# Last edge stage of a four-layer graph network: 144 of its columns built on TensorE instead of 112

## The reference

```
W = jnp.einsum('rb,bio->rio', comp, basis)
msg = node_feats[src] * norm
seg = etype.astype(jnp.int32) * N + dst
s = jax.ops.segment_sum(msg, seg, num_segments=R * N)
h = jnp.einsum('rni,rio->no', s.reshape(R, N, -1), W) + bias
```

## Time and profile before

| | us |
|---|---|
| median of 3 runs (lowest, highest) | 4992.75 (4991.7, 4993.47) |
| profiled execution, its own time | 4994.97 |
| its span, first to last instruction | 4992.8 |
| PE busy | 3904.1 (78%) |
| DVE busy | 4035.4 (81%) |
| ACT busy | 2091.6 (42%) |
| POOL busy | 3669.7 (73%) |
| POOL gathers from `rel_tab`, 672 | 643.1 busy, 205.0 idle in front of them |

### The profile page before, as it was taken

How to read it: one execution, slowest core, us unless ns; L and a number is a source line. 1 busy time by engine, 2 the same in 40 slices (tenths; PEclk the granted TensorE clock), 3 DMA queues, 4 the chain that set the end, 5 groups by cost and what they waited for, 6 DMA issues and landing times. The chain is left out here.

```text
span 4992.8 us, 56860 instructions
## 1 busy us (share of the span) xinstructions
PE 3904.1 (78%) x17000; PEld 2737.1 (55%) x17049; DVE 4035.4 (81%) x5762; ACT 2091.6 (42%) x3734; POOL 3669.7 (73%) x3384
## 2 busy tenths in 40 slices
PE   2788888872999999999999946888883656677651
PEld 1455555542888888888888834333441433333321
DVE  4788889874899999999999956999997647677663
ACT  0577777751344444444444423555554322222221
POOL 6777777764788888888888727777776567777774
PEclk6899999995999999999999957999996778888875
DMA  8788888853788888888888734444443662222221
GB/s 305 248 285 285 286 282 283 283 209 136 285 322 317 324 318 324 316 325 315 325 316 326 277 73 125 136 135 137 135 127 102 265 228 70 66 68 73 66 62 44
DMA packets 359635, 1074.18 MB, mean 215 GB/s; under 512 B 100998, under 2 KB 124354, under 8 KB 315012
## 3 DMA queue, kind: packets, MB, share of 16 engines
q1 hardware_dynamic: 241524, 852.49, 45.8%
q0 software_dynamic: 102208, 156.10, 12.2%
q10 hardware_dynamic: 15696, 63.31, 3.1%
HBM read 678.05 MB, written 392.57 MB: 214 GB/s over the span
## 5 line engine op out<-in xcount | busy, mean ns | idle before, releaser
L1880 PE MATMUL COLS<-CF,XF 128*128 128x256 f32 x6272 | 1485.9, 380 | 6.0 <-DVE XF L1988 6.0
L1880 PEld LDWEIGHTS COLS<-CF,XF 128*128 128x128 f32 x6272 | 1135.1, 190 | 130.2 <-DVE XF L1988 6.4
L1137 ACT ACTIVATE OUT<-SC 128x576 f32<-128x576 f32 (+3 forms) x392 | 577.0, 1472 | 1114.0 <-DVE SC L1072 754.7
L1847 POOL DMA_INDIRECT G<-x_tab,SRC x784 | 835.5, 1066 | 228.9 <-issue 212.6
L1020 POOL DMA_INDIRECT G<-xl_tab,SRC x752 | 721.5, 959 | 229.2 <-issue 224.1
L1020 POOL DMA_INDIRECT G<-rel_tab,REL x672 | 643.1, 957 | 205.0 <-issue 205.0
L1020 POOL DMA_INDIRECT G<-kv_tab,SRC x608 | 601.0, 989 | 193.2 <-issue 172.8
L1457 PE MATMUL PICK<-HOT,X 125*128 125x512 bf16 x2200 | 530.1, 405 | 143.9 <-ACT TURNED L1495 127.2
L1629 PE MATMUL MADE<-XM,W 128*128 128x512 f32 x896 | 486.6, 701 | 162.3 <-DVE XM L1717 162.2
L1457 PEld LDWEIGHTS PICK<-HOT,X 125*128 125x128 bf16 x2200 | 225.1, 103 | 434.3 <-issue 205.3
L1629 PEld LDWEIGHTS MADE<-XM,W 128*128 128x128 f32 x896 | 196.3, 228 | 431.7 <-issue 231.6
(11 more groups left out here) (313 smaller groups left out, 7163.5 us busy)
## 6 DMA issues: line engine op xcount, KB each, us to landing
SHB<-ea9t SPq DMA_DIRECT2D x196, 1024.0 KB, 9.7
wkv_tab<-WKV SPq DMA_DIRECT2D x98, 1024.0 KB, 6.2
WKV<-wkv_tab SPq DMA_DIRECT2D x98, 1024.0 KB, 6.0
scan<-OUT SPq DMA_DIRECT2D x196, 288.0 KB
scan<-OUT ACTq DMA_DIRECT2D x98, 576.0 KB
rel_tab<-YS SPq DMA_DIRECT2D x50, 1024.0 KB
RAW<-spread SPq DMA_DIRECT2D x196, 256.0 KB, 2.8
spread_q<-ZQ SPq DMA_DIRECT2D x98, 512.0 KB
```

What stands on the lines that cost most here:

```text
L1137: nc.scalar.activation(self.OUT[d][:, :, 0:WD], SC[b][:, 0:WD, 1:1 + C].rearrange("p r j -> p j r"), ACT.Copy).then_inc(self.copied_out, 1)
L1847: pool.indirect_dma_start(out=e.G[0][b][:, col, :], out_offset=None, in_=x1_tab, in_offset=bass.IndirectOffsetOnAxis(ap=SRC[:, at:at + 1], ...
L1880: nc.tensor.matmul(acc, XF[b][:, k, edges_], CF[:, k, :], start=(k == 0), stop=False)
```

## The change

Batches become 18 (144 columns, spread over the same 88 chunks, so a batch lasts 5 chunks), and POOL gathers 640 columns instead of 672. The features of 14 batches still come by the gathers into `XG`. Those of the other four (`PICKED3`: batches 5, 9, 13 and 17) are picked by PE: the 1024 source numbers of a batch come in two halves of 512; for a half, ACT makes one-hot rows for 25 node groups in five blocks (`compare`): |number - node| with five activations, then relu(1 - that) with two. PE multiplies each block with the node features held as three bf16 pieces (`pick`: ten bf16 matmuls of 512 columns), ACT copies a half's sum out of PSUM (`take_half`), and `turn` folds the pieces with two f32 matmuls. There are 40 blocks, placed by a table (`PICK_BEFORE`): in groups of four batches 0 to 3, 4 to 7, 8 to 11 and 12 to 15, called A, B, C, D below, with 1, 3, 2 and 4 blocks. Batches 16 and 17 have none.

The weights of 56 chunks, not 64, lie at once in PSUM, beside `MSG`, which frees a PSUM bank for `PICK`; `TYPE8`, `UPPER` and `CODE` have one buffer instead of two. At the stage's start POOL numbers the nodes and clears a part of `X3`, ACT and DVE split the features into three pieces.

```diff
-BATCHES3 = 14
+BATCHES3 = 18
+PICKED3 = [5, 9, 13, 17]
...
+PICK_BEFORE = {16 * (i - 5) + 14 + 5 * g + 4 * (g >= 5): 10 * n + g for n, i in enumerate(PICKED3) for g in range(10)}
...
 def turn(i):
-    wait(pe, doubled, i + 1)
     wait(pe, masked, MASKS * i)
+    if i in PICKED3:
+        wait(pe, half_taken, 2 * PICKED3.index(i) + 2)
+        for h in range(2):
+            ins = nc.tensor.matmul(XT8[:, 512 * h:512 * h + 512],
+                                   FOLD[:, :, :].rearrange("p a f -> p (a f)"),
+                                   PICKED[:, 512 * h:512 * h + 512], start=True, stop=True)
+        ins.then_inc(x_turned, 1)
+        return
...
+def pick(g):
+    h, part = divmod(g, 5)
+    wait(pe, compared, g + 1)
+    if part == 0:
+        wait(pe, half_taken, h)
+    for k in range(5 * part, 5 * part + 5):
+        for piece in range(2):
+            ins = nc.tensor.matmul(PICK[:, :], X3[N, k, piece, :], HOT[g % 2][N, k % 5, :],
+                                   start=(k == 0 and piece == 0),
+                                   stop=(k == K - 1 and piece == 1))
+    ins.then_inc(picked, 1)
...
                 multiply(i, c)
+                if MASKS * i + c in PICK_BEFORE:
...
+                    pick(PICK_BEFORE[MASKS * i + c])
                 if c == 2 and i >= 1:
                     turn_back(i - 1)
...
+def compare(g):
...
+    for n, (k0, m) in enumerate(((0, 3), (3, 2))):
+        wait(act, away_used, 2 * g + n)
+        for a in range(m):
+            k = 5 * part + k0 + a
+            nc.scalar.activation(AWAY[N, a, :], ID16[N, :], ACT.Abs,
+                                 bias=MINUS_NODE[N, k:k + 1]).then_inc(away, 1)
+        wait(act, away, 5 * g + k0 + m)
+        nc.scalar.activation(HOT[g % 2][N, k0:k0 + m, :], AWAY[N, 0:m, :], ACT.Relu,
+                             bias=ONES[N, 0:1], scale=-1.0).then_inc(away_used, 1)
...
                 if t + 1 < NCH:
                     place(t + 1)
+                for g in range(5 * len(HALVES3)):
+                    if t == CHUNK_OF[g]:
+                        compare(g)
...
                 if t == LAST_MASK[i] + 1:
                     take(i)
-                    if i + 2 < BATCHES3:
-                        read_types(i + 2)
+                    if i + 1 < BATCHES3:
+                        read_types(i + 1)
```

More of the change, by code:

```diff
@@ L94 @@
 MADE_COLS = [(t, c) for t in range(NCH) for c in range(C - MADE_IN[t], C)]
+GATHERED3 = [i for i in range(BATCHES3) if i not in PICKED3]
+GATHERED_COLS = [MADE_COLS[8 * i + q] for i in GATHERED3 for q in range(8)]
+HALVES3 = [(i, h) for i in PICKED3 for h in range(2)]
+PICK_BEFORE = {16 * (i - 5) + 14 + 5 * g + 4 * (g >= 5): 10 * n + g for n, i in enumerate(PICKED3) for g in range(10)}
 MADE_AT = [sum(MADE_IN[:t]) for t in range(NCH + 1)]
+CHUNK_OF = {g: max(t for t in range(NCH) if MASKS_AT[t] <= j) for j, g in PICK_BEFORE.items()}
 ROWS3_AT = [sum(C - MADE_IN[q] for q in range(t % 4, t + 1, 4)) for t in range(NCH)]
@@ L695, in _ @@
                         pool.wait_ge(x_stored, 16)
-                        for j, (t, c) in enumerate(MADE_COLS):
+                        for j, (t, c) in enumerate(GATHERED_COLS):
                             at = t * C + c
@@ L857, in __init__ @@
                 else:
-                    self.MSG = (self.wide("MSG", R) if layer > 1 else sb("MSG", [P, R, 1 + C], F32, ctx))
+                    self.MSG = (None if layer > 1 else sb("MSG", [P, R, 1 + C], F32, ctx))
+                if layer == 3:
+                    sums_and_weights = ctx.enter_context(nc.psum_tensor(unique("MSG"), [P, 1024], F32))
+                    self.MSG = sums_and_weights[:, 0:R * (1 + C)].rearrange("p (r j) -> p r j", j=1 + C)
+                    self.EW = sums_and_weights[:, R * (1 + C):R * (1 + C) + 56 * C]
                 if layer == 1:
@@ L1595, in load_types, with load_half @@
                         def load_types(i):
-                            wait(sp, coded, i - 1)
-                            sp.dma_start(TYPE8[i % 2][:, :], type8[i:i + 1, :].to_broadcast([P, 8 * P]))\
-                              .then_inc(type8_in[i % 2], 16)
+                            wait(sp, coded, i)
+                            sp.dma_start(TYPE8[:, :], type8[i:i + 1, :].to_broadcast([P, 8 * P]))\
+                              .then_inc(type8_in, 16)
+                        def load_half(h):
+                            wait(sp, narrowed, h)
+                            sp.dma_start(SRC_HALF[:, :], src_half[h:h + 1, :].to_broadcast([P, 512]))\
+                              .then_inc(src_half_in, 16)
                         load_types(0)
-                        load_types(1)
                         for t in range(NCH):
-                            for i in range(2, BATCHES3):
-                                if t == LAST_MASK[i - 2] + 1:
+                            for i in range(1, BATCHES3):
+                                if t == (LAST_MASK[i - 2] + 1 if i >= 2 else 0):
                                     load_types(i)
+                            for h in range(len(HALVES3)):
+                                if t == (CHUNK_OF[5 * h - 5] if h else 0):
+                                    load_half(h)
                             e.send_rows(sp, t)
@@ L1644, in _ @@
                         wait(pe, weights_made, 4)
+                        wait(pe, folds, 2)
                         for i in range(BATCHES3):
@@ L1649, in _ @@
                                 multiply(i, c)
+                                if MASKS * i + c in PICK_BEFORE:
+                                    if MASKS * i + c == min(PICK_BEFORE):
+                                        wait(pe, blank, 2)
+                                        wait(pe, x_low, 1)
+                                    pick(PICK_BEFORE[MASKS * i + c])
                                 if c == 2 and i >= 1:
@@ L1667, in place, with narrow @@
                                   .then_inc(placed, 1)
-                        wait(act, xg_in, 16 * 8 * BATCHES3)
+                        def narrow(h):
+                            wait(act, src_half_in, (h + 1) * 16)
+                            wait(act, compared, 5 * h)
+                            nc.scalar.activation(ID16[:, :], SRC_HALF[:, :], ACT.Copy).then_inc(narrowed, 1)
+                        def compare(g):
+                            h, part = divmod(g, 5)
+                            if g == 0:
+                                wait(act, negated, 1)
+                                wait(act, x_low, 1)
+                            wait(act, narrowed, h + 1)
+                            wait(act, picked, g - 1)
+                            for n, (k0, m) in enumerate(((0, 3), (3, 2))):
[7 more added lines that the diff above has]
+                                                     bias=ONES[N, 0:1], scale=-1.0).then_inc(away_used, 1)
+                            wait(act, away_used, 2 * g + 2)
+                            act.sem_inc(compared, 1)
@@ new lines, in take_half @@
+                        def take_half(h):
+                            i, half = HALVES3[h]
+                            wait(act, picked, 5 * h + 5)
+                            if h == 0:
+                                wait(act, x_low, 1)
+                            if h >= 2 and half == 0:
+                                wait(act, x_turned, PICKED3[h // 2 - 1] + 1)
+                            nc.scalar.activation(PICKED[:, 512 * half:512 * half + 512], PICK[:, :], ACT.Copy)\
+                              .then_inc(half_taken, 1)
@@ L1670, in _ @@
+                        wait(act, xg_in, 16 * 8 * len(GATHERED3))
                         double(0)
                         double(1)
+                        nc.scalar.activation(X3[:, :, 0, 0:64], X[:, :, :], ACT.Copy).then_inc(x_high, 1)
                         wait(act, e.ready, e.N_READY)
@@ L1676, in step @@
                             for i in range(2, BATCHES3):
-                                if t == LAST_MASK[i - 2] + 2:
+                                if t == LAST_MASK[i - 2] + 2 and i in GATHERED3:
                                     double(i)
+                            if t == 1:
+                                wait(act, x_rest, 1)
+                                nc.scalar.activation(X3[:, :, 0, 64:128], REST, ACT.Copy).then_inc(x_middle, 1)
+                            if t == 1:
+                                narrow(0)
+                            for h in range(len(HALVES3)):
+                                if t == CHUNK_OF[5 * h + 4] + 1:
+                                    take_half(h)
                             if t + 1 < NCH:
                                 place(t + 1)
+                            for g in range(5 * len(HALVES3)):
+                                if t == CHUNK_OF[g]:
+                                    compare(g)
+                                    if g % 5 == 4 and g + 1 < 5 * len(HALVES3):
```

(23 more changed lines are left out.)

57 lines of the change are left out of this document (38 added, 19 removed).

## The result

The changed kernel takes 5045.12 us (4 runs, 5044.04 to 5047.45) against 4992.67 us of the kernel before, a ratio of 1.0106 (95% interval 1.0092 to 1.012): 52 us slower, where 29 were forecast. The way it went was right; the time lies just past the upper end of the range, 5045. The profiled execution has a span of 5043.9 us and took 5045.74.

A forecast was written before the change was run, and what follows sets the result against it. POOL bounds before; afterwards the mask, code and take loop does: first take at 4130.5, sixteen cycles of 724.6 us, then the tail put the stage's end 29 us later, giving 5022 us, range 4990 to 5045.

The forecast's parts named there:

- POOL bounds before, and 32 gathers are worth 40 us: Stage before the change: POOL never pauses, so 32 fewer gathers at 1.26 us are worth up to 40.3 us.
- A gather stays at 1.26 us though DVE gets fuller: POOL's gathers: no stretching from a busier DVE, against the skill page's shared-SBUF rule; 1.26 us each.
- The loop of mask, code and take becomes the bound: DVE and PE per batch: cycles of 43.4 to 46.3 us, all above POOL's 40.3, so POOL waits for buffers.
- Three blocks in PE's path lengthen B and D to 46.3: PE in batches B and D: 39.7 us plus 2.2 for each of three blocks, 46.3 us a cycle.
- The step that failed: ACT's one-hot blocks in batch cycles: DVE delayed at most about 1.3 us a time, taken as 0.
- the term C: Batch C from take to take: two blocks on PE, one filling a 1.4 us wait; 42.7 to 44.1, taken as 43.4 us.
- A turn is 1.73 us: PE's turn at a batch's end: 1.73 us, part of 9.0 us from last mask to take with nothing slow.
- The tail: Stage's end: POOL fills chunk 91 once chunk 87 is summed, then 46 gathers, 58.0 us; stage ends at 4945.5.
- the clock didn't stay high: Rival on PE's clock: it never falls to 0.50, all slow starts go; 4995 us, no change; 17%.
- POOL didn't bound: Rival: mask work overlaps the batch's end better, POOL still bounds; 38.7 us less, 4954 us; 11% including all between.
- ACT's blocks were not late by themselves: Rival on ACT: a block costs 9 us rather than 5.9 and PE waits; about 5090 us; 5%.
- the first rival: PE's clock stays high: cycles A 44.2, B and D 44.6, C 42.0, plain 42.0, sum 699.2; 4995 us; 17%.

The follow-up runs named there:

- 17 batches: Against the kernel before: 17 batches, 648 columns gathered, three batches picked, blocks mostly behind c15 and c11, halves copied one chunk later; 4964.1 us, ratio 0.9947.
- The denser masks: Kernel before with its 14 batches of masks spread over the first 70 chunks, not 88; 672 gathers, no picks; 5010.4 us.
- the blocks elsewhere: Changed kernel with take_half one chunk later and the 40 blocks moved behind c15, c11 and c5, none between turn and take; 5011.6 us.
- the copy moved: Changed kernel with ACT copying each half out of PSUM (take_half) one chunk later, nothing else moved; 5035.2 us.
- the second half's blocks later: 18 batches, late copy, blocks behind c15, c11 and c5, with the second half's five moved to 47, 53, 59, 63, 69 masks; 4982.3 us.

## Why the prediction went as it did

**POOL bounds before, and 32 gathers are worth 40 us:** right. With 17 batches, where POOL hardly pauses, 24 gathers less gave 28.5 us: 24 x 1.26 less the 1.6 at the start is 28.6.

**A gather stays at 1.26 us though DVE gets fuller:** right. It shows with 17 batches, where POOL pauses only once: from the first to the last gather are 818.2 us for 647 steps, 1.26 us each, with DVE busy in 0.78 of that time (before: 0.68).

```profile
4063.33 0.96 POOL L1031 DMA_INDIRECT G<-rel_tab,REL  x1 [0.16 <-issue]
...
4881.52 0.94 POOL L1031 DMA_INDIRECT G<-rel_tab,REL  x1 [0.30 <-issue]
```

**The loop of mask, code and take becomes the bound:** right, shown twice without any block (43.7 and 43.5 us against the forecast 43.5 for a plain batch). The denser masks cost 20 us with all gathers in place.

**Three blocks in PE's path lengthen B and D to 46.3:** right within 0.8 us in the mean (46.7 and 45.6). With the blocks elsewhere one of D's three lies in PE's idle time and one where PE waits for the last mask, and D took 41.4 to 41.8.

**The step that failed** is the cost of ACT in the cycle of C, which was put at nothing: "As factors stand ahead of the block, DVE waits only where two such chunks follow each other [...]. I take 0". It priced the one-hot blocks on ACT and their cover, and left out that `take_half` is a wait too, with the store, the next factors and a place queued behind it. In the C shown above that wait cost 3.1 us on DVE; the term C was 43.4 and measured 47.6, 16.9 us over four, and with the copy moved it measured 44.0, near the term. The range's upper end had 1.3 us for ACT in such batches, for a reason of another kind. The other cycles are off by less and in part cancel: A 4.0 us in sum, B 1.5 and the last one 0.8 longer, D 3.0 shorter; all sixteen are 20.2 longer.

**A turn is 1.73 us:** too short in A, where the folds are matmuls of 512 columns and no transposes. The timeline of one:

```profile
4300.12 3.78 PE L1659 MATMUL XT<-SHARED,FOLD 128*128 128x512 f32 x4 [4.18 <-DVE XM L1834]
4303.70 6.29 PE L1685 MATMUL MADE<-XM,W 128*128 128x512 f32 x12
```

It takes 3.6 us to the next code, with the granted clock from 4300 to 4304 at 0.50. From the last mask to the take A has 13.9 us where the forecast has 12.7, which is most of the 1.3 by which A is longer.

At full clock 1.73 is too long: the turn that it was read from ran at 0.50. In the changed kernel's C and D the granted clock from the turn to the take is 1.00, a turn takes 0.9 us, and the last mask to the take is 8.1 us, not 9.0. That is about the 0.75 by which D is shorter than forecast. Nor had the clock fallen in the idle 7.46 us before the turn at 4461.27, as the prediction has it; it was 0.50 already while PE worked before that, behind an idle of 4.00 us (busy time by stretch, kernel before, columns as the earlier trace rows):

```profile
4450.00:4454.00 4.00, 3.78 (x4) 1.17 (x4) 1.16 (x1) 0.43 (x2) 3.09 (x4) 0.50 0.32 94
```

**The tail:** 96.3 us from the last take but one to the stage's last operation, not 90.4. The forecast lets POOL begin chunk 91 as soon as chunk 87 is summed. But POOL's last pause ends at 4881.5, ahead of chunk 88, and from there it runs unbroken: within a batch DVE does four chunks quicker than POOL fills them, so POOL's lead was not whole at the last mask. Chunk 87 was summed at 4900.2, and POOL came to chunk 91 at 4906.5. Against it stands 3.8 us at the start, 2.7 of them a stage that began earlier in this execution. -3.8 + 20.2 + 5.9 is the 22.3 us that the stage's end (4967.8) lies behind the forecast 4945.5.

```profile
4881.50 0.94 POOL L1030 DMA_INDIRECT G<-rel_tab,REL  x1 [4.40 <-DVE SC L1082]
...
4962.65 0.94 POOL L1030 DMA_INDIRECT G<-rel_tab,REL  x1 [0.30 <-issue]
```

**The rivals:** the clock didn't stay high (0.50 at A's fold, and 7.11 us again for the first three codes after the take at 4126.68). POOL didn't bound. ACT's blocks were not late by themselves: PE never waited for one, and the seven activations of a block took 6.1 us from the first's start to the last's end (4195.15 to 4201.26), forecast 5.9.

**Sums that are off:** the first rival's cycles add up to 699.4 and not 699.2; 40 blocks at 2 us more each give 5102 and not about 5090; the upper end counts eleven batches B, C and D where the sixteen cycles hold twelve, 1.3 us more. None of them changes the forecast of 5022.

## What to carry to other kernels

Where an engine works off a queue in order, every wait put into it delays what stands behind it, also a wait for something cheap: price the wait by when its releaser ends, not by its own length. When work is taken from a bounding engine, work out the cycle of what remains, with its hand-overs, and not its busy time; DVE had 200 us of slack here, and still the loop through it became the bound. Buffers between two engines take up a loop that is a little slower, as long as they are not full: of the counts tried the best one (17 batches) has a loop slightly longer than POOL's time and uses that lead up. The tables of 16, 17 and 18 batches place their blocks differently, so the best count for one placing is not shown.

## What the runs showed that was not expected

A block behind c15 was meant to keep the clock up over the idle time before the next masks. In the run with the blocks elsewhere PE then stood idle for 2.7 us, and the three codes after it took 5.42 us in five cases, but 6.9 to 8.5 in ten:

```profile
4351.18 5.42 PE L1686 MATMUL MADE<-XM,W 128*128 128x512 f32 x12 [2.72 <-DVE XM L1835]
...
4400.95 7.11 PE L1686 MATMUL MADE<-XM,W 128*128 128x512 f32 x12 [2.72 <-DVE XM L1835]
```

The same pause is followed by either speed. The Trainium skill (TensorE: Matmul & The Clock Gate, HAM oscillation) has it that each pause of a loop can throttle the clock. These runs agree: without blocks PE idles 4.9 to 5.3 us there, and none of sixteen groups of three codes ran at full speed (6.8 to 8.2 us); with the block a third did.

More came ahead of the take, and the run without any block shows it. There the last mask to the take is 9.4 to 11.1 us, mean 10.4; in the run with the second half's blocks later it is 8.1 in ten of sixteen cycles, mean 8.8. One batch of each, first without blocks, then a D with a block behind c11; with each the stretch from turn to take, its granted clock third from the end:

```profile
4249.46 1.97 PE L1664 MATMUL XT<-IDENT,X 128*128 128x128 f32 x8 [4.07 <-DVE XM L1822]
4260.32 1.28 DVE L1829 SCALAR_TENSOR_TENSOR TURNED<-UPPER,CODE_OF_F,MADE 128x1024 f32<-128x1024 f32 x1 [8.41 <-PE MADE L1683]
4249.46:4260.32 10.86, 10.76 (x24) 5.34 (x24) 2.42 (x4) 2.69 (x4) 8.37 (x9) 0.74 0.14 27
...
4242.82 2.32 PE L1678 MATMUL PICK<-SHARED,X 125*128 125x512 bf16 x10
4245.03 1.09 PE L1667 MATMUL XT<-IDENT,X 128*128 128x128 f32 x8
4253.09 1.28 DVE L1842 SCALAR_TENSOR_TENSOR TURNED<-UPPER,CODE_OF_F,MADE 128x1024 f32<-128x1024 f32 x1 [4.97 <-PE MADE L1686]
4245.03:4253.09 8.06, 8.06 (x27) 4.02 (x27) 2.57 (x4) 5.36 (x9) 6.20 (x7) 1.00 0.25 63
```

Without blocks PE stood idle for 4.07 us before the turn and the clock from turn to take was 0.74; with them it didn't idle and the clock was 1.00. C, with no block behind c11 and 2.0 us of idle before the turn, has the 8.1 us in three of four cases too, so which of the blocks does it is not shown. But the kernel with all 40 blocks placed so (4982.3 us) is faster than the one with none (5001.5), each by one run and on two chips (the kernel before: 4995.1 and 4990.3): here more work on PE shortened the stretch behind it.
